# A mixture-of-experts kernel: rows of y stored in slot order by SyncE and gathered back by pairs, instead of scattered by GpSimd

## The chip, the cores and the metric

The kernel runs on one core of a Trainium2 chip. The metric is the device time of one execution in microseconds, the median of several. The engines are PE (TensorE), DVE (VectorE), ACT (ScalarE), POOL (GpSimd) and SP (SyncE, which here only issues DMAs).

## The reference

For each of 4 batches of 1024 tokens with 1024 features, a mask is made of the 10240 largest entries of a scaled softmax of x (its diagonal left out). The mask is the input of a mixture of 8 experts; each token goes to its two best experts, and their weighted outputs are added to x.

```python
att = softmax(x, axis=-1) / sqrt(n)
adj = (side * cond) * att            # diagonal set to -inf
m   = 1 where adj is among its 10240 largest, else 0      # [4, 1024, 1024]
scores = softmax(m @ G)              # 8 experts
value, indices = top_k(scores, 2)
w    = sum of value * onehot(indices)
out  = sum_e w_e * ( (silu(m @ gate_e.T) * (m @ up_e.T)) @ down_e.T
                     + (m @ lora_A_e.T) @ lora_B_e.T )
return x + out
```

## The kernel before

A batch is n (0 to 3). The routing of a batch sorts its 2048 pairs (token, expert) by expert into T = 23 tiles of 128 slots; some slots of a tile hold no pair. DVE does the routing (`route`: `choose`, `weigh`, `place_pairs`, `fill_table`, `take_slots`) with two PE steps in it, `rank` and `place_slots`. `choose` waits until the mask of the batch is stored to DRAM.

The tile loop of a batch goes over i = 0 to 22, and each engine has it written out by hand in its own order. For a tile, POOL gathers 128 mask rows of 1 KB from DRAM (`gather`, five tiles ahead, buffers `xg`), PE turns them, ACT unpacks them to `xt`, PE does the first layer, ACT the silu, DVE the gate, PE turns it and does the second layer two iterations later, and ACT scales the result into one of two buffers `y` (`store_y`, line 862), 128 rows of 4 KB in slot order.

Between these steps the loop of batch n carries the mask of batch n + 1: counts on DVE and ACT, `diagonal` on POOL at i = 3 (line 477, after DVE has scaled all rows), `below_third` on POOL at i = 10 to 12 (line 491, waited for by the maxima of DVE), the mask on DVE by i = 17, and its check on DVE in iteration 18, which gives `mask_ready`. After it SP runs `move_mask(n + 1)`: eight loads of x of the batch after that (4 MB) into `v`, then the store of the mask (1 MB). DVE takes a maximum of each of the eight loads in iterations 19 to 22 (`maximum`, line 946), between the gates of the tiles. In batch 2 the loads of `move_mask(3)` are those of x for the last sum, which no maximum waits for.

The output goes back in two steps. `put_out` on POOL (line 529) scatters the tile's 128 rows to `put_rows`, a table in DRAM with a row for each token and role; slots without a pair are skipped. It stands three iterations behind in POOL's order, and ACT may write a `y` buffer again when its scatter has landed. In the loop of batch n + 1, SP loads pieces of 128 tokens by 512 features (x and both roles, 256 KB each) into two buffers, POOL adds them in two instructions (`sum_piece`, lines 538 and 541, 16 pieces, in iterations 1 to 9 and 13 to 19), and SP stores the piece. For the last batch SP loads all rows of both roles in 16 DMAs of 512 KB (line 430), DVE adds them, SP stores.

The waits that hold the two queues together are these:

```python
                act.wait_ge(put[g % NY], 16 * (g // NY))          # L861, before y is written
                pool.wait_ge(y_ready, 2 * (g + 1))                # L528, before a scatter
                sp.wait_ge(summed_piece, u + 1)                   # L382, before a piece is stored
                sp.wait_ge(piece_stored[at], 16 * (u // NC))      # L373, before the next is loaded
```

Of the kernel before, what the change touches and what calls it, by code (L numbers as in the profile page):

```python
# [15 lines left out]
P = 128  # L16
# [18 lines left out]
def build(nc, x, side, cond, G, gate_w, up_w, down_w, lora_A, lora_B, out):  # L35
# [37 lines left out]
    PIECES, NC = 2 * C, 2  # L73
# [29 lines left out]
    PIECE_AT = {**{j + 1: j for j in range(9)}, **{j + 4: j for j in range(9, PIECES)}}  # L103
    PIECES_FIRST = 14

    with ExitStack() as ctx:
# [24 lines left out]
        piece = sb("piece", [P, NC, 3, HALF], F32)  # L131
# [18 lines left out]
        spare = piece[:, :, :, :].rearrange("p i k h -> p (i k h)")  # L150
# [96 lines left out]
        put_row = [table_of(n, 1, I32) for n in range(B)]  # L247
# [30 lines left out]
        put_rows = [nc.dram_tensor(f"put_rows{i}", [ROLES * S, H], F32, kind="Internal").ap() for i in range(2)]  # L278
# [25 lines left out]
        put = [sem(f"put{i}") for i in range(NY)]  # L304
        piece_landed = [sem(f"piece_landed{i}") for i in range(NC)]
        piece_stored = [sem(f"piece_stored{i}") for i in range(NC)]
        half_summed, summed_piece = sem("half_summed"), sem("summed_piece")
# [10 lines left out]
        put_roles = [a.rearrange("(r p c) h -> r p c h", r=ROLES, c=C) for a in put_rows]  # L318
# [15 lines left out]
        def _(sp):  # L334
# [28 lines left out]
            def wait_put(n):  # L363

                for i in range(NY):
                    sp.wait_ge(put[i], 16 * len(range(i, T * (n + 1), NY)))

            def load_piece(n, j):
                u = PIECES * n + j
                at, c, half = u % NC, j // 2, j % 2  # L370
                cols = slice(half * HALF, (half + 1) * HALF)
                if u >= NC:
                    sp.wait_ge(piece_stored[at], 16 * (u // NC))  # L373
                sp.dma_start(piece[:, at, 0, :], x_rows[n][:, c, cols]).then_inc(piece_landed[at], 16)
                for r in range(ROLES):
                    sp.dma_start(piece[:, at, 1 + r, :],
                                 put_roles[n % 2][r][:, c, cols]).then_inc(piece_landed[at], 16)

            def store_piece(n, j):
                u = PIECES * n + j  # L380
                c, half = j // 2, j % 2
                sp.wait_ge(summed_piece, u + 1)  # L382
                sp.dma_start(out_rows[n][:, c, half * HALF:(half + 1) * HALF],
                             piece[:, u % NC, 0, :]).then_inc(piece_stored[u % NC], 16)
# [19 lines left out]
            for n in range(B):  # L404

                more = n + 1 < B
                if n == 0:
                    move_mask(1)
                else:
                    if n == 1:  # L410

                        sp.wait_ge(b_turned, 4)
                        sp.wait_ge(a_turned, 1)
                    wait_put(n - 1)
                    for j in range(PIECES + NC):
                        if j >= NC:
                            store_piece(n - 1, j - NC)
                        if j < PIECES:
                            load_piece(n - 1, j)
                        if more and j == PIECES_FIRST + NC - 1:  # L420
                            move_mask(n + 1)
# [5 lines left out]
            wait_put(n)  # L427
            for c in range(C):
                for r in range(ROLES):
                    sp.dma_start(last_put[c][r], put_roles[n % 2][r][:, c, :]).then_inc(rows_landed[c], 16)  # L430
# [4 lines left out]
            for i in range(NC):  # L435
                sp.wait_ge(piece_stored[i], 16 * len(range(i, PIECES * (B - 1), NC)))

        @block.gpsimd
        def _(pool):
# [86 lines left out]
            def put_out(n, i):  # L526
                g = tile(n, i)
                pool.wait_ge(y_ready, 2 * (g + 1))  # L528
                pool.indirect_dma_start(  # L529
                    out=put_rows[n % 2], out_offset=bass.IndirectOffsetOnAxis(ap=put_row[n][:, i:i + 1], axis=0),  # L530
                    in_=y[:, g % NY, :], in_offset=None,
                    bounds_check=ROLES * S - 1, oob_is_err=False).then_inc(put[g % NY], 16)

            def sum_piece(n, j):
                u = PIECES * n + j
                at = u % NC
                pool.wait_ge(piece_landed[at], 48 * (u // NC + 1))
                nc.gpsimd.tensor_tensor(piece[:, at, 0, :], piece[:, at, 0, :], piece[:, at, 1, :],  # L538
                                        ALU.add).then_inc(half_summed, 1)
                pool.wait_ge(half_summed, u + 1)  # L540
                nc.gpsimd.tensor_tensor(piece[:, at, 0, :], piece[:, at, 0, :], piece[:, at, 2, :],  # L541
                                        ALU.add).then_inc(summed_piece, 1)

            for n in range(B):
# [4 lines left out]
                if n >= 2:  # L549

                    pool.wait_ge(summed_piece, PIECES * (n - 1))
                for i in range(T):
# [4 lines left out]
                    if i >= 3:  # L557
                        put_out(n, i - 3)
# [5 lines left out]
                for i in range(T - 3, T):  # L564
                    put_out(n, i)
# [928 lines left out]
```

## Time and profile before

| What | us |
|---|---|
| median of 3 runs (lowest, highest) | 800.79 (798.49, 806.63) |
| the profiled execution: its time | 801.54 |
| its span, from the first instruction to the last | 799.8 |
| busy: PE, DVE, ACT, POOL | 500.9, 523.6, 442.2, 389.5 |

The profile is of one execution; 1.7 us of its time lie outside the span. Granted TensorE clock: 0.84 of full speed on the mean. The tile loops begin with a first `gather` of their batch; those of batches 1, 2 and 3 begin at 312.15, 472.98 and 641.92 us of the span.

### The profile page before, as it was taken

To read this page: it belongs to the slowest core of one execution; us is meant where nothing else is said; L and a number is where in the kernel's file an instruction comes from. 1 tells how busy PE (TensorE), PEld (TensorE's weight loads), DVE (VectorE), ACT (ScalarE), POOL (GpSimd) and SP (SyncE) were. 2 spreads that over 40 slices of the span, in tenths; PEclk is the share of its full clock that TensorE was granted. 3 is DMA by queue.
4 is the path that set the end of the run, shared out by engine and by line. 5 is a ranking of instruction groups with operands and counts; after the bars stand their busy time and mean duration, and the time that the engine had idled before them with its cause. 6 is when DMAs were issued, how large, how long until landed. Compare 5 with 4: busy or idle time off the path is not lost.

```text
span 799.8 us, 13618 instructions
## 1 busy us (share of the span) xinstructions
PE 500.9 (63%) x3682; PEld 330.4 (41%) x3682; DVE 523.6 (65%) x1242; ACT 442.2 (55%) x655; POOL 389.5 (49%) x337
## 2 busy tenths in 40 slices
PE   0211187259878882788777717977669469788800
PEld 0200076146545551455445414544436246455400
DVE  5768789857598686776786867757872723343245
ACT  6687278738845476297445653973336345455300
POOL 7114200045366123588886136768971177877400
PEclk9755599669999895799999957998988869999865
DMA  9990060013312453368368733575478238767469
GB/s 317 360 269 0 3 261 28 0 49 113 113 74 91 166 217 107 125 226 283 133 220 272 299 102 131 206 261 175 169 252 326 94 102 287 262 207 260 164 259 381
DMA packets 76984, 147.29 MB, mean 184 GB/s; under 512 B 21475, under 2 KB 30699, under 8 KB 76400
## 3 DMA queue, kind: packets, MB, share of 16 engines
q1 hardware_dynamic: 59248, 104.40, 38.4%
q0 software_dynamic: 17664, 41.98, 14.7%
q8 instruction: 39, 0.64, 0.3%
q14 instruction: 33, 0.27, 0.1%
HBM read 95.47 MB, written 69.21 MB: 206 GB/s over the span
## 4 chain that ended last, share of the span: by engine, by line
DVE 20%; DMA 18%; issue 15%; POOL 14%; PE 13%; ACT 8%; DVEq 7%; SPq 2%; POOLq 1%; ACTq 0%
DMA put_rows<-y,where 5%; DMA piece<-put_rows 5%; DMA out_dram<-piece 5%; PE pa L690 4%; DVE mask L1075 4%; ACT mask L805 3%; POOL piece L538 3%; POOL xg L521 3%; DVE small L1037 3%; POOL piece L541 3%; DMA w<-put_rows 2%; ACT y L862 2%; DVEq L1364 2%; DVEq L1031 1%; DVE g_parts L1365 1%
## 5 line engine op out<-in xcount | busy, mean ns | idle before, releaser
L690 PE MATMUL pa<-w,xt 128*128 x1472 | 209.2, 296 | 5.4 <-issue 4.3
L862 ACT ACTIVATE y<-pc,where 128x512 f32<-128x512 f32 x184 | 121.7, 688 | 150.8 <-DMA put_rows<-y,where 94.6
L690 PEld LDWEIGHTS pa<-w,xt 128*128 128x128 f16 x1472 | 149.2, 102 | 74.1 <-issue 25.7
L529 POOL DMA_INDIRECT put_rows<-y,where x92 | 92.1, 1001 | 134.4 <-ACT y L862 114.0
L521 POOL DMA_INDIRECT xg<-mask_rows,where x92 | 99.1, 1078 | 115.8 <-DVEq L1349 95.0
L1357 DVE SCALAR_TENSOR_TENSOR g_full<-pa,where,s_act 128x144 f32<-128x144 f32 x92 | 33.5, 364 | 177.2 <-ACT s_act L854 177.2
L849 ACT ACTIVATE xt<-pb 128x1024 f16<-128x1024 uint8 x92 | 94.2, 1024 | 46.7 <-PE pb L677 46.5
L713 PE MATMUL pc<-wd,gt 128*128 x184 | 75.6, 411 | 13.1 <-ACT y L862 11.9
L714 PE MATMUL pc<-wd,gt 128*128 x184 | 75.9, 413 | 0.0
L715 PE MATMUL pc<-wd,gt 128*128 x184 | 75.5, 410 | 0.0
L716 PE MATMUL pc<-lb,gt 128*128 x184 | 75.5, 410 | 0.0
L538 POOL TENSOR_TENSOR piece<-piece 128x512 f32<-128x512 f32 x48 | 61.2, 1275 | 26.6 <-DMA piece<-put_rows 25.9
L854 ACT ACTIVATE s_act<-pa,small 128x128 f32<-128x128 f32 x92 | 33.9, 369 | 68.9 <-PE pa L690 68.7
L805 ACT ACTIVATE mask<-v,small 128x1280 f16<-128x1280 f32 x48 | 65.3, 1360 | 7.1 <-POOL v L477 3.9
L541 POOL TENSOR_TENSOR piece<-piece 128x512 f32<-128x512 f32 x48 | 62.5, 1302 | 3.8
L1365 DVE TENSOR_TENSOR g_parts<-g_full,g_parts 128x144 f16<-128x144 f32 x92 | 53.7, 583 | 7.2 <-issue 0.4
L677 PE MATMUL pb<-ident,xg 128*128 128x128 f16 x368 | 37.7, 228 | 26.9 <-issue 15.8
L701 PE MATMUL pb<-ident,g_parts 128*128 128x128 f16 x276 | 31.5, 225 | 32.5 <-DVE gt L1373 32.5
L1019 DVE TENSOR_SCALAR_CACHE_REDUCE mask<-v,small 128x1024 f16<-128x1024 f32 x36 | 44.9, 1272 | 2.7 <-POOL v L477 2.1
L946 DVE TENSOR_REDUCE small<-v 128x1 f32<-128x1024 f32 x32 | 38.5, 1214 | 11.3 <-DMA v<-in_x_dram 11.0
L966 DVE SCALAR_TENSOR_TENSOR v<-v,small,t_row 128x1024 f32<-128x1024 f32 x32 | 43.8, 1408 | 0.6
L491 POOL TENSOR_TENSOR t_row<-v,mask 128x1024 f32<-128x1024 f32 x12 | 25.6, 2131 | 30.3 <-PE pm L583 21.5
(208 smaller groups left out, 864.9 us busy)
## 6 DMA issues: line engine op xcount, KB each, us to landing
piece<-put_rows SPq DMA_DIRECT2D x96, 256.0 KB, 3.9
v<-in_x_dram SPq DMA_DIRECT2D x40, 512.0 KB, 8.5
piece<-in_x_dram SPq DMA_DIRECT2D x48, 256.0 KB, 2.9
out_dram<-piece SPq DMA_DIRECT2D x48, 256.0 KB
w<-put_rows SPq DMA_DIRECT2D x16, 512.0 KB, 9.6
w<-in_L_ffn_gate_w_dram SPq DMA_DIRECT2D x8, 512.0 KB, 10.3
w<-in_L_ffn_up_w_dram SPq DMA_DIRECT2D x8, 512.0 KB, 8.3
wd<-in_L_ffn_down_w_dram SPq DMA_DIRECT2D x8, 512.0 KB, 9.5
```

What stands on the lines that cost most here:

```text
L521: pool.indirect_dma_start(out=xg[:, g % NX, :], out_offset=None, in_=mask_rows[n % 2], in_offset=bass.IndirectOffsetOnAxis(ap=mask_row[n][ ...
L529: pool.indirect_dma_start(out=put_rows[n % 2], out_offset=bass.IndirectOffsetOnAxis(ap=put_row[n][:, i:i + 1], axis=0), in_=y[:, g % NY, : ...
L538: nc.gpsimd.tensor_tensor(piece[:, at, 0, :], piece[:, at, 0, :], piece[:, at, 1, :], ALU.add).then_inc(half_summed, 1)
L541: nc.gpsimd.tensor_tensor(piece[:, at, 0, :], piece[:, at, 0, :], piece[:, at, 2, :], ALU.add).then_inc(summed_piece, 1)
L690: last = pe.matmul(l1[g % 2], xt[:, g % 2, t, :], w1[:, bass.ds(e, 1), t, k, :].rearrange("p o n -> p (o n)"), start=(t == 0 and k == 0), ...
L713: pe.matmul(pc[:, half, :], high, own(wd[:, bass.ds(e, 1), 0, cols]), start=True, stop=False)
L714: pe.matmul(pc[:, half, :], high, own(wd[:, bass.ds(e, 1), 1, cols]), start=False, stop=False)
L715: pe.matmul(pc[:, half, :], low, own(wd[:, bass.ds(e, 1), 0, cols]), start=False, stop=False)
L716: pe.matmul(pc[:, half, :], lora, own(lb[:, bass.ds(e, 1), cols]), start=False, stop=True).then_inc(y_done, 1)
L805: nc.scalar.activation(mask[:, cols], v_flat[:, cols], ACT.Sign, bias=t_at[k - 1], scale=-1.0, accum_out=act_cnt[:, p:p + 1]).then_inc(act ...
L849: nc.scalar.activation(parts_in(xt[:, g % 2, :, :]), bytes_of(xt_ps), ACT.Copy).then_inc(xt_ready, 1)
L862: nc.scalar.activation(y[:, g % NY, half * HALF:(half + 1) * HALF], pc[:, half, :], ACT.Copy, scale=y_scale[n][:, i:i + 1]).then_inc(y_rea ...
```

## The change

`y` goes to DRAM as it lies: SP stores each tile's 128 rows of 4 KB in slot order to `y_rows` (`store_tile`), three iterations behind in SP's loop, and ACT waits for that store before it writes the buffer again. `put_out` is gone from POOL. DVE keeps the slot of each pair (`pair_slot`) in place of the rows of the scatter. In the loop of the next batch POOL gathers, for 128 tokens and one role, 128 rows of 4 KB by their slots into the one buffer `piece[:, NC, :]` (`gather_pair`), and adds them to x in `piece` in one instruction of 128x1024 an iteration later (`add_pair`). There are 16 of each a batch. A new gather follows the addition of the one before it. SP loads and stores x and the sums in 128x1024 pieces; its stores, its loads and `move_mask` now stand in one loop with `store_tile`, `move_mask` behind the last store of a piece, in iteration 21. For the last batch POOL issues 16 gathers where SP issued 16 loads.

```diff
-    PIECE_AT = {**{j + 1: j for j in range(9)}, **{j + 4: j for j in range(9, PIECES)}}
-    PIECES_FIRST = 14
+    PAIR_AT = {**{k: k for k in range(9)}, **{k + 4: k for k in range(9, Q)}}
+    ADD_AT = {i + 1: k for i, k in PAIR_AT.items()}
+    STORE_OUT_AT = {i + 2: k // ROLES for i, k in PAIR_AT.items() if k % ROLES}
+    LOAD_X_AT = {i + 1: c + NC for i, c in STORE_OUT_AT.items() if c + NC < C}
+    NEXT_X_AT = 21
...
-        piece = sb("piece", [P, NC, 3, HALF], F32)
+        piece = sb("piece", [P, NC + 1, H], F32)
...
+            def store_tile(n, i):
+                g = tile(n, i)
+                sp.wait_ge(y_ready, 2 * (g + 1))
+                if i == 0 and n >= 2:
+                    sp.wait_ge(pair_added, Q * (n - 1))
+                sp.dma_start(y_rows[n % 2][i * P:(i + 1) * P, :], y[:, g % NY, :]).then_inc(y_stored[g % NY], 16)
...
+            def store_piece(n, c):
+                u = C * n + c
+                sp.wait_ge(pair_added, ROLES * (u + 1))
+                sp.dma_start(out_rows[n][:, c, :], piece[:, u % NC, :]).then_inc(piece_stored[u % NC], 16)
...
+                if n > 0:
+                    for c in range(NC):
+                        load_piece(n - 1, c)
+                for i in range(T):
+                    if n > 0 and i in STORE_OUT_AT:
+                        store_piece(n - 1, STORE_OUT_AT[i])
+                    if n > 0 and i in LOAD_X_AT:
+                        load_piece(n - 1, LOAD_X_AT[i])
+                    if n + 1 < B and i == NEXT_X_AT:
+                        move_mask(n + 1)
+                    if i >= BACK:
+                        store_tile(n, i - BACK)
+                for i in range(T - BACK, T):
+                    store_tile(n, i)
...
+            def gather_pair(n, k):
+                u = Q * n + k
+                if u > 0:
+                    pool.wait_ge(pair_added, u)
                 pool.indirect_dma_start(
+                    out=piece[:, NC, :], out_offset=None, in_=y_rows[n % 2],
+                    in_offset=bass.IndirectOffsetOnAxis(ap=pair_slot[n][:, k:k + 1], axis=0),
+                    bounds_check=T * P - 1, oob_is_err=False).then_inc(pair_landed, 16)
+
+            def add_pair(n, k):
+                u, v_of = Q * n + k, C * n + k // ROLES
+                pool.wait_ge(pair_landed, 16 * (u + 1))
+                if k % ROLES == 0:
+                    pool.wait_ge(piece_landed[v_of % NC], 16 * (v_of // NC + 1))
+                else:
+                    pool.wait_ge(pair_added, u)
+                nc.gpsimd.tensor_tensor(piece[:, v_of % NC, :], piece[:, v_of % NC, :], piece[:, NC, :],
+                                        ALU.add).then_inc(pair_added, 1)
...
                     if i + NX < T:
                         gather(n, i + NX)
-                    if i >= 3:
-                        put_out(n, i - 3)
+                    if n > 0 and i in ADD_AT:
+                        add_pair(n - 1, ADD_AT[i])
+                    if n > 0 and i in PAIR_AT:
+                        if PAIR_AT[i] == 0:
+                            wait_stored(n - 1)
+                        gather_pair(n - 1, PAIR_AT[i])
...
-                    act.wait_ge(put[g % NY], 16 * (g // NY))
+                    act.wait_ge(y_stored[g % NY], 16 * (g // NY))
...
+                if n >= 2:
+                    dve.wait_ge(pair_added, Q * (n - 1))
+                V.tensor_copy(pair_slot[n], slot)
...
-                V.tensor_copy(put_row[n], none_here)
```

## Rows read from the trace of the kernel before

**Rows 1.** The page's costliest groups: busy, mean ns of one | idle before, releaser

```profile
L862 ACT ACTIVATE y<-pc,where 128x512 f32<-128x512 f32 x184 | 121.7, 688 | 150.8 <-DMA put_rows<-y,where 94.6
...
L538 POOL TENSOR_TENSOR piece<-piece 128x512 f32<-128x512 f32 x48 | 61.2, 1275 | 26.6 <-DMA piece<-put_rows 25.9
...
L491 POOL TENSOR_TENSOR t_row<-v,mask 128x1024 f32<-128x1024 f32 x12 | 25.6, 2131 | 30.3 <-PE pm L583 21.5
```

**Rows 2.** ACT's timeline, batch 3: start, length, what: the silu of two following tiles

```profile
656.92 0.37 ACT L854 ACTIVATE s_act<-pa,small 128x128 f32<-128x128 f32 x1 [1.37 <-PE pa L690]
...
660.93 0.37 ACT L854 ACTIVATE s_act<-pa,small 128x128 f32<-128x128 f32 x1 [1.20 <-PE pa L690]
```

**Rows 3.** POOL's timeline, batch 3: iteration 0's gather, later one whole iteration

```profile
648.50 1.00 POOL L521 DMA_INDIRECT xg<-mask_rows,where  x1 [0.30 <-issue]
...
684.28 1.26 POOL L538 TENSOR_TENSOR piece<-piece 128x512 f32<-128x512 f32 x1 [0.57 <-DMA piece<-put_rows]
...
687.02 1.04 POOL L521 DMA_INDIRECT xg<-mask_rows,where  x1
688.37 1.00 POOL L529 DMA_INDIRECT put_rows<-y,where  x1 [0.30 <-issue]
689.72 1.26 POOL L538 TENSOR_TENSOR piece<-piece 128x512 f32<-128x512 f32 x1 [0.34 <-DMA piece<-put_rows]
```

**Rows 4.** DMA issues of batch 1's stretch (311 to 470 us), median us to landing

```profile
xg<-mask_rows,where POOLq DMA_INDIRECT x23, 3.1
put_rows<-y,where POOLq DMA_INDIRECT x23, 3.8
```

**Rows 5.** The same view of batch 3's stretch (640 to 765 us)

```profile
xg<-mask_rows,where POOLq DMA_INDIRECT x23, 3.7
put_rows<-y,where POOLq DMA_INDIRECT x23, 4.3
```

**Rows 6.** POOL's timeline, batch 1: diagonal, first below third, iteration 13's gather

```profile
337.30 2.03 POOL L477 TENSOR_SCALAR_AFFINE_SELECT v<-v 128x1024 f32<-128x1024 f32 x1 [8.89 <-DVE v L966]
...
381.76 2.13 POOL L491 TENSOR_TENSOR t_row<-v,mask 128x1024 f32<-128x1024 f32 x1
...
399.10 1.06 POOL L521 DMA_INDIRECT xg<-mask_rows,where  x1 [0.16 <-issue]
```

**Rows 7.** POOL's timeline, batch 2: diagonal and first below third

```profile
497.87 2.05 POOL L477 TENSOR_SCALAR_AFFINE_SELECT v<-v 128x1024 f32<-128x1024 f32 x1 [6.88 <-DVE v L966]
...
546.15 2.13 POOL L491 TENSOR_TENSOR t_row<-v,mask 128x1024 f32<-128x1024 f32 x1
```

**Rows 8.** SP's timeline: the loads of x in batches 0, 1, 2; batch 1's mask

```profile
270.77 4.55 SPq L337 DMA_DIRECT2D v<-in_x_dram  x8
...
431.86 4.66 SPq L337 DMA_DIRECT2D v<-in_x_dram  x8
436.57 0.59 SPq L398 DMA_DIRECT2D mask_rows<-mask  x1
...
599.21 3.96 SPq L394 DMA_DIRECT2D v<-in_x_dram  x8
```

**Rows 9.** The page's DMA issues, all batches: count, KB each, median us to landing

```profile
mask_rows<-mask SPq DMA_DIRECT2D x4, 1024.0 KB, 14.4
```

**Rows 10.** ACT's timeline, end of batch 0: tile 17's y

```profile
277.08 1.28 ACT L862 ACTIVATE y<-pc,where 128x512 f32<-128x512 f32 x2
```

**Rows 11.** DVE's timeline: first maxima in batch 0; the beginning of `choose` in batches 1, 2

```profile
276.78 2.33 DVE L946 TENSOR_REDUCE small<-v 128x1 f32<-128x1024 f32 x2
...
453.39 0.35 DVE L1238 TENSOR_REDUCE mask<-pm 128x64 f32<-128x192 f32 x1
...
622.60 0.35 DVE L1238 TENSOR_REDUCE mask<-pm 128x64 f32<-128x192 f32 x1
```

**Rows 12.** The chain that ended last, at the end of batch 1

```profile
432.72 9.96 DMA put_rows<-y,where
```

**Rows 13.** SP's timeline, behind the last tile

```profile
766.26 8.24 SPq L430 DMA_DIRECT2D w<-put_rows  x16
```

More of the change, by code:

```diff
@@ L149, in build @@
         raw_down = [wd[:, e, :, :].rearrange("p q h -> p (q h)").bitcast(F32) for e in range(E)]
-        spare = piece[:, :, :, :].rearrange("p i k h -> p (i k h)")
+        spare = piece[:, :, :].rearrange("p i h -> p (i h)")
         raw_A = spare[:, 0:H]
@@ L246, in build @@
         mask_row = [table_of(n, 0, I32) for n in range(B)]
-        put_row = [table_of(n, 1, I32) for n in range(B)]
+        pair_slot = [table_of(n, 1, I32)[:, 0:Q] for n in range(B)]
         g_scale = [table_of(n, 2) for n in range(B)]
@@ L361, in _, with load_piece @@
                 sp.dma_start(raw_B[:, e, :, :], lora_B_apart[e]).then_inc(b_again, 16)
[L363 to L371, printed above, removed]
-                if u >= NC:
[L373 to L384, printed above, removed]
+            def store_tile(n, i):
[4 more added lines that the diff above has]
+                sp.dma_start(y_rows[n % 2][i * P:(i + 1) * P, :], y[:, g % NY, :]).then_inc(y_stored[g % NY], 16)
+            def load_piece(n, c):
+                u = C * n + c
+                if u >= NC:
+                    sp.wait_ge(piece_stored[u % NC], 16 * (u // NC))
+                sp.dma_start(piece[:, u % NC, :], x_rows[n][:, c, :]).then_inc(piece_landed[u % NC], 16)
+            def store_piece(n, c):
+                u = C * n + c
+                sp.wait_ge(pair_added, ROLES * (u + 1))
+                sp.dma_start(out_rows[n][:, c, :], piece[:, u % NC, :]).then_inc(piece_stored[u % NC], 16)
             def move_mask(n):
@@ L404, in _ @@
             for n in range(B):
[L406 to L421, printed above, removed]
+                if n == 1:
+                    sp.wait_ge(b_turned, 4)
+                    sp.wait_ge(a_turned, 1)
+                if n > 0:
[12 more added lines that the diff above has]
+                    store_tile(n, i)
                 if n + 2 < B:
@@ L524, in gather, with wait_stored @@
                     bounds_check=S - 1, oob_is_err=False).then_inc(gathered[g % NX], 16)
-            def put_out(n, i):
-                g = tile(n, i)
-                pool.wait_ge(y_ready, 2 * (g + 1))
-                pool.indirect_dma_start(
[L530 to L542, printed above, removed]
+            def wait_stored(n):
+                for i in range(NY):
+                    pool.wait_ge(y_stored[i], 16 * len(range(i, T * (n + 1), NY)))
+            def gather_pair(n, k):
+                u = Q * n + k
+                if u > 0:
+                    pool.wait_ge(pair_added, u)
+                pool.indirect_dma_start(
+                    out=piece[:, NC, :], out_offset=None, in_=y_rows[n % 2],
[10 more added lines that the diff above has]
+                                        ALU.add).then_inc(pair_added, 1)
             for n in range(B):
@@ L561, in _ @@
                             below_third(n + 1, q)
-                    if n > 0 and i in PIECE_AT:
-                        sum_piece(n - 1, PIECE_AT[i])
-                for i in range(T - 3, T):
-                    put_out(n, i)
+            n = B - 1
+            wait_stored(n)
+            for c in range(C):
+                for r in range(ROLES):
+                    pool.indirect_dma_start(
+                        out=last_put[c][r], out_offset=None, in_=y_rows[n % 2],
+                        in_offset=bass.IndirectOffsetOnAxis(ap=pair_slot[n][:, ROLES * c + r:ROLES * c + r + 1],
+                                                            axis=0),
+                        bounds_check=T * P - 1, oob_is_err=False).then_inc(rows_landed[c], 16)
         @block.tensor
```

18 lines of the change are left out of this document (6 added, 12 removed).

## The prediction

> **What bounds the kernel now.** I read the costliest groups first. ACT's writes of y wait for the scatter of the buffer, 94.6 us in all [rows 1], so the way of y to DRAM matters. The timelines say where. In batch 3, which carries no mask work, two tiles that nothing hinders are 4.0 us apart on ACT [rows 2]. A little later POOL's iterations are 5.4 us apart from one first sum to the next [rows 3]: two sums of 1.27, a gather of mask rows and a scatter at 1.35 from start to start, and 0.3 to 0.6 of waiting for a piece. All tiles then go at POOL's pace, because a scatter stands behind the sums in POOL's order. In batches 1 and 2, POOL's first `below_third` follows at once on its ninth piece [rows 6, 7], and the mask of the next batch follows on that. Last, the loads of x in `move_mask` and the maxima that wait for them set the end of batches 0 and 1, with a slow scatter of 9.96 us beside them [rows 8, 11, 12]. So there are three places to price: POOL's period while it combines, the moment at which `move_mask` runs, and the release of y at a batch's end.
>
> **The pair step.** POOL loses 92 scatters and 28 us of issue on balance (64 gathers come in). It also loses the waits for y. But the new combination is serial: `gather_pair(k)` waits for the addition of k - 1, there is one buffer, and the addition waits for the gather's landing. The step is the landing L, the addition A, and 0.2 of handing over (the gap ahead of a DMA issue is 0.15 to 0.3 [rows 3]). The gather of mask rows in the same iteration, 1.3, lies within L and costs nothing.
>
> A is not in the trace. Its bounds: 2.13 for 128x1024 with a half-width operand, and twice 1.275 = 2.55 for two sums of 512 columns [rows 1]. I take 2.4, nearer to the upper one, whose operands are the same.
>
> L is not in the trace either. Gathers of at most 128 KB land 3.1 us after their issue in batch 1 and 3.7 in batch 3 [rows 4, 5]. Scatters land after 3.8 and 4.3, with 2048 of 2944 rows filled, so 356 KB of 512 on the mean. Between the two kinds lie about 0.6 us for 267 KB; another 156 KB are 0.4. I take 4.3 for batches 1 and 2 and 4.8 for batch 3, the scatter's rows rather than the gather's, since the size is nearer. The bounds are 3.1, if only rows and not bytes count, and about 5.8, if the fuller store of y (512 KB in place of 356) and the gather crowd each other as those of batch 3 did, and once more.
>
> So a step is 4.3 + 2.4 + 0.2 = 6.9 us in batches 1 and 2, and 7.4 in batch 3, against 5.4 before. By the bounds it lies between 5.4 and 8.5.
>
> **Batch 0** has no pairs. But `move_mask(1)` now stands at iteration 21 of SP, behind the store of tile 17. That tile's y is ready at 277.08 + 1.28 = 278.4 [rows 10], and the loads went out at 270.77 [rows 8]: 7.6 us later. DVE began the first maxima at 276.78 [rows 11], 6 us after the issue; now the first load lands at about 278.8 + 4. The gates of tiles 20 to 22 stand behind these maxima. DVE had about 2 us to spare. I book +5 (0 to 8).
>
> **Batch 1.** Two pairs fit ahead of `diagonal`, as two pieces did, and the third gather lands beside it. `diagonal` ends at 339.3 [rows 6]; 1.2 for a gather and 2.4 for the addition give 343.0; six steps of 6.9 give 384.4; 1.3 for the gather of iteration 10, and `below_third` begins at 385.7, not 381.76: 4 us late. From there to the gather of iteration 13 it took 17.3 us [rows 6]. Two scatters of 1.3 leave this stretch, one more mask gather comes in before the pair, and DVE's share stays; I take 17, so pair 9 goes out at 402.7. Seven steps, 48.3, and pair 15 is added at 451.0. Here is the largest term. SP stores the last piece in iteration 21 and only then runs `move_mask`: the loads of x go out at 451.4, not at 431.86 [rows 8], where they followed the mask at once. DVE's maxima, the gates behind them and `choose` follow the loads as before, 21.5 us on [rows 8, 11]. +19.
>
> In the same iteration tile 18 is stored behind the 4 MB of loads and the 1 MB of the mask. The mask itself lands 14.4 us after its issue behind such loads [rows 9]; the store of y must land about 15 us late as well, where the scatter, on the other queue, took 9.96 [rows 12]. That sets y of tile 20, and by it `rank`, which is wanted some 7 us after `choose`; it fits, so I price it at 0 here (up to 5 where it doesn't).
> The Trainium skill (DMA: Bandwidth & Descriptors, Queues, rings and completion order) says that each DMA engine takes a queue's descriptors in ring order and goes round between queues packet by packet. By this rule moving y onto SP's queue costs what I say; were the two queues one pool, tile 18 would land as the scatter did, and the sum would be the same, since this term is at 0.
>
> **Batch 2.** `diagonal` ends at 499.9 [rows 7]; the same 3.6 + 41.4 + 1.3 give 546.3 for `below_third`, against 546.15: nothing. Then 17 + 48.3, and pair 15 is added at 611.6, so `move_mask(3)` runs at 612.0, not 599.21 [rows 8]. No maximum waits for these loads, but `choose` waits for the mask: 612.0 + 4.0 for the issues + 14.4 [rows 9] = 630.4, against 622.60 [rows 11]. +8.
>
> **Batch 3.** The sixth gather ends at 649.5 [rows 3]. Nine steps of 7.4 from 649.8 give 716.4, four gathers of 1.3 give 721.7, seven steps give 773.5. PE could be far ahead (23 tiles of 4.0 are 92 us), but SP stores tile 18 only after piece 7, that is after 773.9. It lands about 4.0 later (a scatter's 3.8 to 4.3, [rows 4, 5]), ACT writes tile 20 in 1.3, its store takes 4.4, ACT writes tile 22, its store takes 4.4: 789.4. Before, the rows were all there at 766.26 [rows 13]. +23. Sixteen gathers at 1.3 are 21 us of issue where SP's loads took 8.24; both are within the 23 us in which 8 MB come in, but for the last: +1.
>
> **The rest at nothing.** DVE exchanges one small copy for another and a wait for additions that ended an iteration earlier. The waits of ACT for a scatter go, but what is late next in the combining iterations is SP, whose store of y stands behind `store_piece`, so behind the same addition. In the iterations without pairs the tiles go at PE's or DVE's pace; that gives a few us in batch 0, where DVE leads anyway.
>
> **The sum:** 5 + 19 + 8 + 24 = 56 on a span of 799.8, 855.8, and 1.7 outside it: 857.5 against 801.54. The median before is 0.75 lower than that execution: 857.
>
> **The rivals.**
> - *Shorter landings.* L at 3.5 makes the step 6.1. Batch 1: 13 steps that count, 10 us less, +9; batch 2 then runs its mask in time, 0; batch 3: 16 steps by 1.3, +3; batch 0: +5. 818. For it: the gather lands on chip as the mask rows do, and these are quicker than the scatters [rows 4]. Against: four times the bytes. The Trainium skill (DMA: Bandwidth & Descriptors, Anatomy of one DMA) puts most of the fixed 2 us on the receipt of the last write, and most of all for HBM. By it this case gains; the trace has no pair of equal size to show it.
> - *Faster: y is released early and POOL keeps up.* Place: the combining iterations of batch 3. If a step is no longer than the 5.4 us of before, POOL needs 16 x 5.4 + 7 x 1.3 = 95 us for 23 tiles, about PE's 92, and SP stores y at once. ACT's waits go, batch 3 loses some 18 us, batches 1 and 2 some 3 each, batch 0 costs 5: 782. For it: those 94.6 us of waits [rows 1]. Against: it decides at a step of 5.4, and the lower bound of my step is just that.
> - *No change.* A step of 5.7 or so, where losses at the ends and gains in the loops cancel: 800. That POOL's relief is real but falls on a chain that SP holds just as fast would look the same.
> - *Longer landings.* L at 5.8 in all batches: 26 steps by 1.5 and 16 by 1.0 on top, 912. For it: y is stored in full, and the gathers meet it.
>
> **How the numbers follow.** The main case, a step of 6.5 to 7.7 us, has 0.55, and by itself reaches from 832 to 890. Shorter landings 0.23, longer 0.05, no change 0.07, faster 0.10. The range must take in the shorter landings and most of the longer: 806 to 897 leaves out the faster case, most of no change and a part of the longest, 0.19 together. A change of 1% is about what this measurement can tell from none. Faster by over 1%: 0.10; within 1%: 0.07; slower: 0.83.
>
> **What the profile after would show.** POOL's `add_pair` waits for the gather in nearly every one of 48; their starts are about 7 us apart; the mean of an addition is 2.4. The loads of x in batch 1 come straight after the store of the last piece, some 20 us after `mask_ready`, and DVE's maxima wait for them. The store of tile 18 lands over 10 us after its issue in batches 0 to 2. ACT still waits for y buffers. I am wrong if gathers of 512 KB land within 3.5 us, if the addition is nearer to 2, or if POOL reaches iteration 20 before DVE has the mask ready.

## The result and the profile after

The changed kernel took 958.35 us (median of 4 runs, 953.21 to 963.25), against 799.64 for the one before beside it: a ratio of 1.196, interval 1.186 to 1.206. The forecast was 857, with a range of 806 to 897. The direction was right and the size was not: 159 us more, where 57 were forecast.

The page of the changed kernel, its costliest groups (columns as in [rows 1], whose first and second line the first two here answer to):

```profile
L868 ACT ACTIVATE y<-pc,where 128x512 f32<-128x512 f32 x184 | 122.2, 687 | 294.3 <-DMA y_rows<-y 189.9
...
L540 POOL TENSOR_TENSOR piece<-piece 128x1024 f32<-128x1024 f32 x48 | 116.2, 2420 | 183.6 <-DMA piece<-y_rows,where 183.6
...
L952 DVE TENSOR_REDUCE small<-v 128x1 f32<-128x1024 f32 x32 | 38.5, 1213 | 48.9 <-DMA v<-in_x_dram 48.4
```

ACT now waits 189.9 us for the way of y to DRAM, twice the 94.6 of before. The addition costs what was forecast (2.42 on the mean), but POOL waits 183.6 us for the 48 gathers ahead of it. That is more than the gathers' issue, the additions or any other work on POOL.

POOL's timeline in batch 1, after `diagonal` (start, length, what, idle before and releaser); it answers to [rows 3, 6]:

```profile
350.20 1.02 POOL L528 DMA_INDIRECT piece<-y_rows,where  x1 [0.77 <-POOL piece L540]
...
354.70 2.36 POOL L540 TENSOR_TENSOR piece<-piece 128x1024 f32<-128x1024 f32 x1 [2.17 <-DMA piece<-y_rows,where]
357.83 1.02 POOL L528 DMA_INDIRECT piece<-y_rows,where  x1 [0.77 <-POOL piece L540]
...
365.61 2.34 POOL L540 TENSOR_TENSOR piece<-piece 128x1024 f32<-128x1024 f32 x1 [5.46 <-DMA piece<-y_rows,where]
368.71 1.02 POOL L528 DMA_INDIRECT piece<-y_rows,where  x1 [0.77 <-POOL piece L540]
...
373.29 2.34 POOL L540 TENSOR_TENSOR piece<-piece 128x1024 f32<-128x1024 f32 x1 [2.26 <-DMA piece<-y_rows,where]
...
403.15 2.34 POOL L540 TENSOR_TENSOR piece<-piece 128x1024 f32<-128x1024 f32 x1 [5.83 <-DMA piece<-y_rows,where]
405.64 1.02 POOL L515 DMA_INDIRECT xg<-mask_rows,where  x1
406.69 2.13 POOL L485 TENSOR_TENSOR t_row<-v,mask 128x1024 f32<-128x1024 f32 x1
...
425.74 1.00 POOL L528 DMA_INDIRECT piece<-y_rows,where  x1 [0.31 <-issue]
```

Read the distance from each issue to the addition that it releases. 350.20 to 354.70 is 4.5 us; 357.83 to 365.61 is 7.8; 368.71 to 373.29 is 4.6 again. Gathers of one size land in two ways by turns (in all of batch 1 after 4.3 to 5.2 us and after 6.8 to 8.2), so steps of 7.6 and 11 us alternate. The second thing is the 0.77 us between an addition's end and the next issue, where the issue waits for that addition; at 405.64 a gather of mask rows, which doesn't wait for the addition ending at 405.49, follows 0.15 after.

SP's timeline over the same stretch and at the end of batch 1, which answers to [rows 8]:

```profile
357.09 0.34 SPq L382 DMA_DIRECT2D out_dram<-piece  x1
357.47 0.43 SPq L371 DMA_DIRECT2D y_rows<-y  x1
359.74 0.33 SPq L377 DMA_DIRECT2D piece<-in_x_dram  x1
360.12 0.46 SPq L371 DMA_DIRECT2D y_rows<-y  x1
...
487.67 0.34 SPq L382 DMA_DIRECT2D out_dram<-piece  x1
488.05 0.43 SPq L343 DMA_DIRECT2D small<-in_fside_BxSx_dram  x1
488.52 4.53 SPq L340 DMA_DIRECT2D v<-in_x_dram  x8
```

The gather of 357.83 is the long one. Around it SP, held until then by `store_piece`, lets go four DMAs of 512 KB within 3 us: a sum, two tiles of y and a load of x. The same addition that lets POOL issue the next gather lets SP start this burst. At 487.67 the last sum is stored, and only behind it come the loads of x, 488.52 where they were at 431.86. What waited for them, on DVE (it answers to [rows 11]):

```profile
492.64 2.58 DVE L952 TENSOR_REDUCE small<-v 128x1 f32<-128x1024 f32 x2 [32.09 <-DMA v<-in_x_dram]
...
506.98 0.34 DVE L1244 TENSOR_REDUCE mask<-pm 128x64 f32<-128x192 f32 x1
```

32.09 us of DVE's time stood open for them, with the gates of tiles 20 to 22 behind; `choose` began at 506.98 instead of 453.39. The landing of the stores of y behind the mask, from a stretch at the end of batch 0 (280.8 to 290 us; issues and median us to landing):

```profile
y_rows<-y SPq DMA_DIRECT2D x2, 512.0 KB, 13.3
```

By batches, from the first gather of mask rows to the next batch's (batch 3: to the first load of the last rows; the tail from there to the span's end), all from the timelines:

| us | up to batch 1 | batch 1 | batch 2 | batch 3 | tail |
|---|---|---|---|---|---|
| before | 312.2 | 160.8 | 168.9 | 124.3 | 33.5 |
| after | 314.3 | 213.5 | 215.1 | 176.6 | 39.2 |
| difference | +2 | +53 | +46 | +52 | +6 |
| forecast | +5 | +19 | +8 | +23 | +1 |

### The profile page after: what moved, and what is told of

It is laid out like the page before. It is cut to its first block and busy times, and to the rows that moved or that the text cites. A ratio compares the mean times of both kernels' runs of the same rounds, so it can differ in the third digit from the quotient of the medians.

```text
span 958.8 us, 13494 instructions
## 1 busy us (share of the span) xinstructions
PE 524.7 (55%) x3682; PEld 339.9 (35%) x3682; DVE 521.4 (54%) x1242; ACT 442.4 (46%) x655; POOL 351.8 (37%) x261
## 5 line engine op out<-in xcount | busy, mean ns | idle before, releaser
L868 ACT ACTIVATE y<-pc,where 128x512 f32<-128x512 f32 x184 | 122.2, 687 | 294.3 <-DMA y_rows<-y 189.9
L515 POOL DMA_INDIRECT xg<-mask_rows,where x92 | 94.1, 1023 | 251.8 <-DVEq L1357 207.8
L540 POOL TENSOR_TENSOR piece<-piece 128x1024 f32<-128x1024 f32 x48 | 116.2, 2420 | 183.6 <-DMA piece<-y_rows,where 183.6
L719 PE MATMUL pc<-wd,gt 128*128 x184 | 81.2, 441 | 88.1 <-ACT y L868 87.9
L720 PE MATMUL pc<-wd,gt 128*128 x184 | 81.5, 443 | 0.0
L721 PE MATMUL pc<-wd,gt 128*128 x184 | 81.0, 440 | 0.0
L722 PE MATMUL pc<-lb,gt 128*128 x184 | 79.9, 434 | 0.0
L528 POOL DMA_INDIRECT piece<-y_rows,where x48 | 49.9, 1040 | 36.7 <-POOL piece L540 27.7
L1373 DVE TENSOR_TENSOR g_parts<-g_full,g_parts 128x144 f16<-128x144 f32 x92 | 58.6, 637 | 7.2 <-issue 0.4
L683 PE MATMUL pb<-ident,xg 128*128 128x128 f16 x368 | 37.8, 229 | 39.2 <-DMA xg<-mask_rows,where 21.4
L719 PEld LDWEIGHTS pc<-wd,gt 128*128 128x128 f16 x184 | 19.8, 107 | 109.7 <-issue 100.4
L707 PEld LDWEIGHTS pb<-ident,g_parts 128*128 128x128 f16 x276 | 18.9, 99 | 73.7 <-issue 72.4
## 6 DMA issues: line engine op xcount, KB each, us to landing
mask_rows<-mask SPq DMA_DIRECT2D x4, 1024.0 KB, 12.6
```

Source lines behind the costliest of these rows:

```text
L515: pool.indirect_dma_start(out=xg[:, g % NX, :], out_offset=None, in_=mask_rows[n % 2], in_offset=bass.IndirectOffsetOnAxis(ap=mask_row[n][ ...
L540: nc.gpsimd.tensor_tensor(piece[:, v_of % NC, :], piece[:, v_of % NC, :], piece[:, NC, :], ALU.add).then_inc(pair_added, 1)
L707: last = pe.transpose(gt_ps[:, k, :], g_parts[:, g % 2, at:at + P], ident[:, :])
L719: pe.matmul(pc[:, half, :], high, own(wd[:, bass.ds(e, 1), 0, cols]), start=True, stop=False)
L720: pe.matmul(pc[:, half, :], high, own(wd[:, bass.ds(e, 1), 1, cols]), start=False, stop=False)
L721: pe.matmul(pc[:, half, :], low, own(wd[:, bass.ds(e, 1), 0, cols]), start=False, stop=False)
```

## The experiments

There are twelve runs, and beside them the kernel before took 799.2, 802.7 and 802.7 us. `c6` and `c5` are medians of four and ten executions, all others single ones; the four of the changed kernel lie 10 us apart, so a few us between two single runs mean nothing. The mean step is the distance between the starts of following additions of pairs in batch 3, the pause in iterations 9 to 12 left out. The table gives the changed kernel and the eleven runs made from it; `c5`, made from the kernel before, stands at the end.

| run | us | batch 1 | batch 3 | mean step |
|---|---|---|---|---|
| after | 958.4 | 213.5 | 176.6 | 9.6 |
| e1_small_y | 905.4 | 198.4 | 155.0 | 8.2 |
| e5_no_gather | 803.6 | 164.3 | 109.8 | (3.9, no gather) |
| e3_early_mask | 942.9 | 204.7 | 178.2 | 9.7 |
| e4_y_on_act | 899.5 | 203.5 | 147.3 | 8.6 |
| e2_two_gathers | 894.7 | 194.9 | 149.3 | 7.7 |
| e6_y_on_pool | 910.2 | 197.7 | 161.7 | 8.0 |
| c4_early_act | 860.3 | 176.9 | 149.1 | 8.6 |
| c2_two_early_act | 862.4 | 183.3 | 141.0 | 8.1 |
| e7_rotate | 841.1 | 171.6 | 134.7 | 6.2 |
| c6_rotate_early_act | 826.0 | 166.0 | 132.3 | 6.7 |
| e8_floor | 790.2 | 161.4 | 109.5 | (no gather) |

### Why every other gather lands late

`e1_small_y`:

```diff
-                sp.dma_start(y_rows[n % 2][i * P:(i + 1) * P, :], y[:, g % NY, :]).then_inc(y_stored[g % NY], 16)
+                sp.dma_start(y_rows[n % 2][i * P:(i + 1) * P, 0:P], y[:, g % NY, 0:P]).then_inc(y_stored[g % NY], 16)
...
-                    out=piece[:, NC, :], out_offset=None, in_=y_rows[n % 2],
+                    out=piece[:, NC, :], out_offset=None, in_=x.rearrange("b s h -> (b s) h"),
```

> Edit: the store of each tile's y moves 128 of 1024 columns (64 KB in place of 512), and all gathers of pairs read the same slots from x instead of from the stored rows, so that output is not the sum asked for; every instruction, wait and gather size stays. In the changed kernel pair steps alternate between 7.6 and 11.0 us, because every other gather lands after about 7.8 us and the others after 4.4. Theory (contention): the long ones meet a burst of SP's DMAs (a sum's store, two stores of y, a load of x, 2 MB within 3 us), so with 0.9 MB less in the burst the long landing falls to 5.5 to 6.5 us, the step's mean from 9.35 to about 8.4, and the time from 958 to about 905 to 920. Rival (order alone): the alternation comes from SP's and POOL's waits and not from bytes; the landings stay at 4.4 and 7.8 and the time at 945 to 958.

It took 905.4 us. POOL's timeline at the same place as above:

```profile
354.26 1.01 POOL L528 DMA_INDIRECT piece<-in_x_dram,where  x1 [0.80 <-POOL piece L540]
...
360.27 2.34 POOL L540 TENSOR_TENSOR piece<-piece 128x1024 f32<-128x1024 f32 x1 [3.70 <-DMA piece<-in_x_dram,where]
363.41 1.01 POOL L528 DMA_INDIRECT piece<-in_x_dram,where  x1 [0.80 <-POOL piece L540]
...
367.87 2.34 POOL L540 TENSOR_TENSOR piece<-piece 128x1024 f32<-128x1024 f32 x1 [2.14 <-DMA piece<-in_x_dram,where]
```

The long landing fell from 7.8 to 6.0 us here (354.26 to 360.27), which is the longest of its batch; the others of its kind took 4.9 to 5.6. The short one stayed at 4.5, so reading the rows from x instead of from `y_rows` didn't change a gather that meets no burst. Every wait and every issue was as before. So the bytes of y make most of the difference between the two landings, and the rival of mere order, by which they stay at 4.4 and 7.8, is out. The 0.8 us that are left on the mean weren't tried apart.

### What the gathers cost in all

`e5_no_gather`:

```diff
-                pool.indirect_dma_start(
-                    out=piece[:, NC, :], out_offset=None, in_=y_rows[n % 2],
...
-                pool.wait_ge(pair_landed, 16 * (u + 1))
...
-                nc.gpsimd.tensor_tensor(piece[:, v_of % NC, :], piece[:, v_of % NC, :], piece[:, NC, :],
+                nc.gpsimd.tensor_tensor(piece[:, v_of % NC, :], piece[:, v_of % NC, :], piece[:, v_of % NC, :],
```

> Edit: in batches 0 to 2 the gathers of pairs are left out, and each addition adds the piece to itself, so the output lacks y there; stores of y by SP, additions, loads and stores of pieces, move_mask and the last batch's 16 gathers stay. Theory (landing): what costs is that POOL waits for each gather; without it a step is 1.3 + 2.4, POOL is ahead of DVE and PE, move_mask runs at mask_ready or at tile 17's y, and the time falls to 765 to 800. Rival (SP's order and ring): y behind other DMAs on one queue costs of itself; then the tiles still wait for buffers in the combining iterations, and the time stays over 830.

803.6 us: 155 of the 159 us are gone with the gathers of three batches. It is a little above the range that I gave for the theory (765 to 800), and far below the rival's 830. The row of its last gathers shows that batch 3 ends there 109.8 us after its first gather (653.46), 14 us less than before, and POOL had long been idle:

```profile
763.26 1.01 POOL L563 DMA_INDIRECT w<-y_rows,where  x1 [24.36 <-DMA y_rows<-y]
```

So y on SP's queue isn't dear of itself. But the gain of batch 3 was spent elsewhere: 3.5 and 6 us in batches 1 and 2, 2 in batch 0, 5 in the tail. Even with gathers that cost nothing, the change as written saves nothing.

### The two doors: SP's order and the place of the mask

`e3_early_mask`:

```diff
-    NEXT_X_AT = 21
+    NEXT_X_AT = 19
...
+                    if n + 1 < B and i == NEXT_X_AT:
+                        move_mask(n + 1)
                     if n > 0 and i in STORE_OUT_AT:
                         store_piece(n - 1, STORE_OUT_AT[i])
                     if n > 0 and i in LOAD_X_AT:
                         load_piece(n - 1, LOAD_X_AT[i])
-                    if n + 1 < B and i == NEXT_X_AT:
-                        move_mask(n + 1)
```

> Edit: move_mask stands in iteration 19 of SP, ahead of the store of that iteration's piece, instead of iteration 21 behind the last one. In the changed kernel the loads of x go out at 488.5 in batch 1, where the mask is ready at about 453. If the loads of x set the end of batch 1, they go out some 30 us earlier and the maxima don't wait; but the stores of tiles 16 and 18 still stand behind the additions of pairs 13 and 15, so by the theory (the additions hold y too) the batches 1 and 2 gain about 12 us each and batch 0 about 4: 925 to 935. Rival (only the mask's place costs at the ends): 30 us in batch 1, 20 in batch 2: 900 to 908.

942.9 us, 15 less and near neither. The loads of x in batch 1 went out at 459.59 instead of 488.52, 29 us earlier, and the batch became 9 us shorter. The stores of tiles 16 and 18 still waited for the additions of pairs 13 and 15, as the theory has it. It had put 12 us each for batches 1 and 2, where 9 and 13 came. Its 4 us of batch 0 didn't come (2 us longer instead), and batch 3, which the edit leaves alone, came out 1.6 us longer.

`e4_y_on_act`, where SP's `store_tile` issues nothing:

```diff
             def store_y(n, i, half):
...
+                if half == 1:
+                    act.wait_ge(y_ready, 2 * (g + 1))
+                    if i == 0 and n >= 2:
+                        act.wait_ge(pair_added, Q * (n - 1))
+                    act.dma_start(y_rows[n % 2][i * P:(i + 1) * P, :], y[:, g % NY, :]).then_inc(y_stored[g % NY], 16)
```

> Edit: ACT itself issues the store of a tile's y, on its own queue, right after it has written it; nothing else changes. Theory (the pair steps hold the tiles through two doors, SP's order and POOL's gathers of mask rows): with SP's door open the tiles of the combining iterations run ahead until POOL's gathers of mask rows, five tiles ahead, hold them; batch 3 ends when POOL's iteration 17 is done plus about 15 us, 20 to 25 us earlier; batches 1 and 2 keep the loads of x behind pair 15 and gain 5 to 10 each: 915 to 930. Rival (SP's lock is the whole loss): the tiles go at 4 to 6 us, and 158 us of loss shrink by more than half, under 880.

899.5 us, 59 less, between the two. Batch 3 came down by 29 us. The wait for y buffers is gone; ACT now waits for PE, and PE for the gathers of mask rows behind POOL's steps:

```profile
ACT y L865 <- PE pc L719: 131.1, 98, 27.0
...
PEld pb L680 <- DMA xg<-mask_rows,where: 42.7, 17, 6.0
```

(the view of all waits: engine and line, releaser, us in total, times, longest). Two things were mended at once: the lock, and the burst, from which the stores of y were gone; the mean step fell from 9.6 to 8.6. By 15 steps the second is about 15 of the 29 us; they weren't tried apart.

`c4_early_act` has both edits.

> Edit: move_mask in SP's iteration 19, and y stored by ACT on its own queue, together. Alone they took 15 and 59 us off the 958. With y no longer behind the additions, the early loads of x can now count in full in batches 1 and 2 (they went out about 20 us behind the mask there): theory 860 to 885. Rival: the two gains are the same one, 895 to 900.

860.3 us: 98 less, where the two alone gave 15 and 59. Behind the additions each of them was covered by the other, so the early mask is worth 39 us once y is free, 27 of them in batch 1. The theory's range holds it.

### The other half of the change alone

`e6_y_on_pool`, where SP's `store_tile` issues nothing either:

```diff
+            def put_out(n, i):
+                g = tile(n, i)
+                pool.wait_ge(y_ready, 2 * (g + 1))
+                if i == 0 and n >= 2:
+                    pool.wait_ge(pair_added, Q * (n - 1))
+                pool.dma_start(y_rows[n % 2][i * P:(i + 1) * P, :], y[:, g % NY, :]).then_inc(y_stored[g % NY], 16)
...
+                    if i >= 3:
+                        put_out(n, i - 3)
```

> Edit: only the second half of the change: y is stored in slot order, but by POOL, where the scatter stood (three iterations behind); the combination by gathers stays as changed. Theory (the loss is that of the pair steps, with the release of y tied to them by whichever queue): the tiles stay tied to POOL's steps, now directly; the store's 1.3 us of POOL lies within the gather's landing, the burst of SP loses its stores of y, and the time is 900 to 945. Rival (the place of y on SP is the larger loss): 860 or less, as with y on ACT's own queue and better.

910.2 us, inside the theory's range. POOL's timeline in batch 1:

```profile
352.68 1.06 POOL L532 DMA_INDIRECT piece<-y_rows,where  x1 [0.77 <-POOL piece L544]
354.04 1.00 POOL L512 DMA_INDIRECT xg<-mask_rows,where  x1 [0.30 <-issue]
355.05 0.57 POOL L522 DMA_DIRECT2D y_rows<-y  x1
357.50 2.34 POOL L544 TENSOR_TENSOR piece<-piece 128x1024 f32<-128x1024 f32 x1 [1.88 <-DMA piece<-y_rows,where]
360.62 1.04 POOL L532 DMA_INDIRECT piece<-y_rows,where  x1 [0.77 <-POOL piece L544]
```

Now the gathers land by no turns: after 4.4 to 5.6 us in batch 1, 4.8 on the mean, and the steps behind the first two are 7.5 to 8.3. The bytes are still there. The gather issued at 368.30 lands after 4.6 us although SP stores a sum at 367.56 and loads x at 370.20, and POOL stores y at 370.67, each 512 KB, 1.5 MB within 3.1 us. What differs from the burst is that y comes one tile at a time, 2.4 us behind the gather and on the gather's own queue. Which of these spares the gather no run shows. The kernel is still 108 us slower than the run before beside it. So the combination by gathers with one buffer is the dear half, and y on SP (in the burst, and behind SP's waits) makes it dearer by 48.

### Can the landing be hidden?

`e2_two_gathers` deals the three buffers out as one for x and two for gathers:

```diff
-    NC = 2
+    NC = 1
...
-                if u > 0:
-                    pool.wait_ge(pair_added, u)
+                if u > 1:
+                    pool.wait_ge(pair_added, u - 1)
...
-                    out=piece[:, NC, :], out_offset=None, in_=y_rows[n % 2],
+                    out=piece[:, NC + u % 2, :], out_offset=None, in_=y_rows[n % 2],
```

> Edit: the three 4 KB buffers of the combination are dealt out otherwise: two for gathers, so that the gather of pair k goes out before pair k - 1 is added, and one for x (in place of two), whose next load follows the store of its sum. SP's order and the place of move_mask stay. Theory (the serial step of gather, landing and addition is the loss): for two pairs there now follow a store of a sum 2.3 us, a load of x about 4, and two additions of 2.4 with 0.8 between them, 11.5 to 12.5 us where it was 18.7; 42 steps by 3.1 to 3.6 us shorter take 130 to 150 us off, 810 to 830. Rival (DMA traffic is the bound): the landings lengthen as the gathers crowd, and the time stays over 880.

894.7 us: the theory missed, and the rival's time came, but not by its mechanism. The gathers hold next to nothing: POOL waited 5.5 us in all for them, and 114.8 for x. POOL's timeline shows one such wait:

```profile
366.16 2.36 POOL L540 TENSOR_TENSOR piece<-piece 128x1024 f32<-128x1024 f32 x1
...
376.93 2.34 POOL L540 TENSOR_TENSOR piece<-piece 128x1024 f32<-128x1024 f32 x1 [5.94 <-DMA piece<-in_x_dram]
```

and SP's, between the two:

```profile
368.55 0.34 SPq L382 DMA_DIRECT2D out_dram<-piece  x1
371.22 0.33 SPq L377 DMA_DIRECT2D piece<-in_x_dram  x1
371.60 1.24 SPq L371 DMA_DIRECT2D y_rows<-y  x2
```

Store, load and landing of x are 8.4 us from the end of one addition to the next, in series, and the load meets two stores of y. One serial chain was exchanged for another: 15.6 us for two steps where I had reckoned 12, in part because I took the load at 4 us and it landed in 5.7. That much of the rival's traffic is there.

`c2_two_early_act`, with the early mask and y on ACT added:

> Edit: all three together: two buffers for gathers and one for x, move_mask in SP's iteration 19, y stored by ACT. Theory: the steps are near 6 us, nothing else waits for them, and what is left is what the kernel without gathers showed: 795 to 815. Rival (traffic): over 840.

862.4 us, on the rival's side. POOL waited 150.8 us for x, 36 more than in `e2`. Between `c4` and this one the gathers' wait was exchanged for that of x at no gain.

`e7_rotate` adds the two gathered rows first and x last, and moves the roles of the buffers on by one with each piece:

```diff
+                nc.gpsimd.tensor_tensor(piece[:, g % 3, :], piece[:, g % 3, :], piece[:, (g + 1) % 3, :],
+                                        ALU.add).then_inc(pair_added, 1)
+                pool.wait_ge(pair_added, 2 * g + 1)
+                pool.wait_ge(piece_landed[0], 16 * (g + 1))
+                nc.gpsimd.tensor_tensor(piece[:, g % 3, :], piece[:, g % 3, :], piece[:, (g + 2) % 3, :],
+                                        ALU.add).then_inc(pair_added, 1)
```

> Edit: the same three buffers, but each sum begins with the two gathered rows and takes x last, and the buffers change roles from piece to piece, so that a load of x has two additions and a landing to hide behind; both gathers of a piece go out together. SP's order, its stores of y and move_mask's place stay. The run with two gather buffers left 15.6 us for two steps, of which 8.1 were a store and the next load of x. Theory (the serial step): two steps fall to 11 to 13 us, a step to 5.5 to 6.5, and the time to 835 to 865, with SP's lock and the late mask left. Rival (traffic): two gathers at once land as late as one in a burst, 8 us, two steps stay near 15 and the time near 890.

841.1 us, in the theory's range, with a mean step of 5.9 in batch 1 and 6.2 in batch 3. SP still stores y, and `move_mask` still stands in iteration 21. SP's order moved a little with the sums: each load of x now follows its store at once, and the last four sums are stored an iteration earlier. With that, the shorter steps gave back 117 of the 159 us.

`c6_rotate_early_act`, with all three edits:

> Edit: the rotation of the three buffers, move_mask in iteration 19, and y stored by ACT. Theory: nothing of the changed kernel's loss is left but the gathers' own issue, and it comes to 795 to 815, by the kernel without gathers (804) less what the early mask gives. Rival: the traffic of gathers still holds POOL in batch 3, 830 to 845.

826.0 us, ratio to before 1.030, interval 1.024 to 1.036. The theory's range ended at 815, the rival's began at 830. POOL's timeline in batch 3:

```profile
685.64 1.02 POOL L526 DMA_INDIRECT piece<-y_rows,where  x1
686.96 1.00 POOL L526 DMA_INDIRECT piece<-y_rows,where  x1 [0.30 <-issue]
...
694.73 2.34 POOL L535 TENSOR_TENSOR piece<-piece 128x1024 f32<-128x1024 f32 x1 [4.07 <-DMA piece<-y_rows,where]
697.75 2.35 POOL L539 TENSOR_TENSOR piece<-piece 128x1024 f32<-128x1024 f32 x1 [0.69 <-DMA piece<-in_x_dram]
```

Two gathers, issued 1.3 us apart just behind a store of y and one of a sum, land 7.8 us after the second; in batches 1 to 3 such pairs that POOL waited for took 5.5 to 9.9. Two steps cost 14 us here and 12 in batch 1. I put that down to the tiles' pace, since each tile of batch 3 brings its 512 KB of y sooner; no run shows it.

`e8_floor` is this design's bound: no gathers, early mask, y on ACT.

> Edit: the gathers of batches 0 to 2 left out as in the first such run (the output lacks y there), and move_mask in iteration 19 and y stored by ACT besides. It bounds what the changed design can reach if its gathers cost nothing. Theory: 785 to 798, since the run without gathers had its loads of x some 5 us late in batches 1 and 2; rival: those batches are DVE's, and it stays at 800 to 804.

790.2 us, as the theory had it. Batch 3 takes 109.5 us; batches 1 and 2 take 161.4 and 165.9, about what they took before (160.8 and 168.9). By this one run the way of combining could win about 1.5%, if its gathers were free.

### The kernel before with DVE's help

`c5_before_dve_sums`, the kernel before with the sums of batch 3's loop on DVE:

```diff
-                    if n > 0 and i in PIECE_AT:
+                    if 0 < n < B - 1 and i in PIECE_AT:
                         sum_piece(n - 1, PIECE_AT[i])
...
             # on DVE, after store_gt in each iteration
+                    if n == B - 1 and i in PIECE_AT:
+                        sum_piece(n - 1, PIECE_AT[i])
```

> The kernel before, with one edit: in the loop of batch 3, where DVE is busy 38 of 124 us, DVE and not POOL adds the pieces, at the same iterations. The kernel without gathers showed batch 3 at 110 us where POOL's sums and scatters had made it 124. Theory (POOL's period of 5.4 holds the tiles of batch 3): POOL's iteration falls to 2.7 us, and the tiles go at 4.0 to 4.6: 783 to 792. Rival (the y buffers and the landing of the scatter hold them, or DVE's waits for pieces hold the gates): 797 to 803.

806.5 us, ratio 1.005 (1.002 to 1.008): not faster, and beyond both ranges. Batch 3 took 132.1 us (639.28 to 771.43), 8 more. Its group on DVE:

```profile
L1372 DVE TENSOR_TENSOR piece<-piece 128x512 f32<-128x512 f32 x16 | 11.0, 689 | 41.8 <-DMA piece<-put_rows 41.8
```

The sums are cheap there, two times 11 us in all, but DVE waits 41.8 us for pieces, in order, and each tile's gate stands behind such a wait. POOL waited less for its pieces, 25.9 us over 48 sums [rows 1], against 41.8 over 16 here. No version tried that puts out the whole sum beats the kernel before.

## Why the prediction was wrong

**The step that failed** is "So a step is 4.3 + 2.4 + 0.2 = 6.9 us in batches 1 and 2, and 7.4 in batch 3". It measured 9.4, 9.5 and 9.6 in batches 1, 2 and 3. Of its three terms:
- A, 2.4: measured 2.34 to 2.42. Right.
- The handing over, 0.2: measured 0.77. I took the gap ahead of a DMA issue from rows in which the issue waited for nothing of POOL's own [rows 3]. Here it waits for the semaphore of the addition just ahead, and the trace of before has no such pair. That is 0.6 of each step.
- L, 4.3 (4.8 in batch 3): measured 4.5 and 7.8 by turns, 6.1 on the mean of batch 1. The value for a gather left alone was right. What I left out is that the addition which lets a gather go also lets SP's queue go. `e1` shows that the bytes of y are most of the cause, and `e6` that the landing stays at 4.8 on the mean when y isn't in the burst. I had priced the crowding at up to 5.8, from the slower rows of batch 3 [rows 5], as a mean traffic and not as a meeting.

**The rest of the sum stood.** Put the measured steps in, and my own path gives batch 1: 19 + 13 x 2.46 = 51 (measured 53); batch 2: 8 + 13 x 2.55 = 41 (46); batch 3: 23 + 14 x 2.2 = 54 (52). So the two couplings were right: the pair steps hold the tiles through SP's order, and hold `move_mask`. `e4` and `c4` show them from the other side, by 59 and 98 us. In batch 3 only 14 of the 16 steps grew: the first and the one over the pause (12.6 us, as forecast) took what I had put. The longest step that I allowed was 8.5, and the rival that came near it gave 912; the range ended at 897, short even of that, and the measured steps passed both.

PE's granted clock was lower after, too: 0.80 of full speed on the mean of batch 3 against 0.93, with PE busy 112.5 us instead of 102.9. As the measured steps carry the sum by themselves, I take little of the loss to be these 9.6 us, but no run sets them apart.

**Batch 0, +5:** measured +2. Tile 17's y was ready at 274.25, not at 278.4 as before, so the loads of x went out at 275.11, 4.3 us late and not 7.6; `choose` began 0.9 us late. **The stores of y behind the mask:** tile 18's landed 13.3 us after its issue, where I had said about 15 late; ACT waited 1.8 us for it in batch 0 and 2.7 in batch 1, and pricing it near 0 was right there. In batch 2 it didn't fit: ACT wrote tile 20's y only at 720.85, its exponentials for the routing (L904) stand behind that, and DVE waited for them:

```profile
727.70 0.23 DVE L1271 TENSOR_TENSOR mask<-mask 128x64 f32<-128x64 f32 x1 [4.33 <-ACT mask L904]
```

These 4.3 us, within the "up to 5 where it doesn't" that I named and priced at 0, are most of what batch 2 lies above 41. The 13.3 us agree with the Trainium skill's rule of ring order (DMA: Bandwidth & Descriptors, Queues, rings and completion order), but one pool for both queues could give them too. In `e4` the store of y at the same place, on ACT's queue at 279.25 and 2 us behind the mask's issue on SP's, had landed by 287.91, after 8.7 us; that speaks for the rule. **The tail, +1:** measured +6; the tail is 37.9 to 39.4 us against 33.5 in all runs with POOL's gathers of the last rows. I had compared the issues, 21 us, with the 23 us of the transfer; that they run into each other at the start and the end I had put at 1. This wasn't tried apart.

**The rivals.** Faster needed a step of 5.4; the shortest of the changed kernel was 7.3, though `e5` shows that the place was right: batch 3 falls to 110 us when POOL is out of the way. Shorter landings, for which I had cited the Trainium skill on receipts from HBM (DMA: Bandwidth & Descriptors, Anatomy of one DMA), didn't come. The pair of equal size that I missed is there in `e6`, on POOL's own queue. A gather of 512 KB from DRAM took about 4.5 us at its shortest, and a store of 512 KB to DRAM less, in batch 0 where little else moved (200 to 240 us; count, KB each, median us to landing):

```profile
y_rows<-y POOLq DMA_DIRECT2D x6, 512.0 KB, 3.0
```

So in this kernel the receipt from HBM doesn't make the gather the quicker one. Longer landings had the right sign and too small a chance, 0.05. Even its L of 5.8 lies below the measured 6.1, and it shares the handing over of 0.2, which makes some 23 of the 46 us from its 912 to 958.

## What to carry to other kernels

When one event releases work on two queues, the two transfers meet each time; price the second one's landing in the burst, not by its median over the trace. A chain of gather, landing, addition and next gather through one buffer costs its whole length at each step, and what stands behind it on another engine's queue pays it too: draw that chain first, and only then count the instructions saved. Two repairs behind the same wait look small one by one (15 and 59 us) and are worth more together (98).

## What the runs showed of the hardware

- POOL's issue of a DMA that waits for POOL's own addition just ahead begins 0.77 us after that addition's end (0.80 in `e1`), where an issue without such a wait begins after 0.15.
- A gather of 128 rows of 4 KB by POOL landed mostly 4.3 to 4.7 us after its issue when no burst met it. It took 4.9 to 6.0 beside four DMAs of together 1.1 MB that SP issued within 3 us (`e1`), and mostly 7.6 to 8.2 beside four of 2 MB. In `e6` it took 4.6 beside 1 MB from SP with a store of 512 KB behind it on its own queue.
- Two such gathers 1.3 us apart, just behind two stores, landed 7.8 us after the second (`c6`, batch 3).
- A store of 512 KB to DRAM landed 2.6 us after its issue by SP (the sums, median) and 3.0 by POOL (`e6`, batch 0).
- POOL adds two 128x1024 f32 tiles in 2.34 us, 0.2 less than two additions of 128x512 at 1.275 each [rows 1].
